# Mixture-of-experts layer on one core: full expert tiles first, each expert's last tile after them, and the padding rows written during the expert phase

## The reference

```
x = x + cross_attention(layernorm(x), ctx)
xf = layernorm(x)
scores = softmax(xf @ gate_w.T)               # 32 experts
tw, ti = top_k(scores, 4);  tw /= tw.sum()    # 4 experts for each token
rg, ru = xf @ Rg.T, xf @ Ru.T
for e in range(32):                           # only the tokens that chose e count
    g = silu(rg @ Ug[e].T @ Cg[e].T);  u = ru @ Uu[e].T @ Cu[e].T
    y += w_e * ((g * u) @ Rd.T @ Ud[e].T @ Cd[e].T)
x = x + y + shared_expert(xf)
```

## Time and profile before

| | |
|---|---|
| time, median of 3 runs | 877.85 us (876.92 to 878.13) |
| time of the profiled execution | 878.0 us |
| its span, first to last instruction | 876.3 us |
| PE busy, share of the span | 777.2 us, 89% |
| POOL busy, DVE busy | 482.0 us, 593.4 us |
| first block | 0 to 407.3 us |
| expert phase, then combine phase | from 407.4 us to some 752 us, then to 876.3 us |

### The profile page before, as it was taken

The page is one execution under the profiler, slowest core; times in us unless marked ns, Lnnn a source line. Parts: engine busy times, 40 slices in busy tenths (PEclk is TensorE's granted clock), DMA queues, the critical chain, the costliest instruction groups (busy, mean ns, idle before and its releaser), DMA issues.

```text
span 876.3 us, 22261 instructions
## 1 busy us (share of the span) xinstructions
PE 777.2 (89%) x6034; PEld 639.1 (73%) x6035; DVE 593.4 (68%) x2017; ACT 469.4 (54%) x1411; POOL 482.0 (55%) x684
## 2 busy tenths in 40 slices
PE   4899999999999999632999999999999999999995
PEld 2566666666666666422898998899899898888884
DVE  2578888888888888540565666566566566477887
ACT  2678888888888888411444444444444443322331
POOL 0126566666666666570455555555555556576665
PEclk9999999999999999855999999999999999999998
DMA  6345655555555555776344444344344342577875
GB/s 193 101 121 168 177 168 172 178 169 178 175 167 169 172 172 178 236 193 180 116 132 127 123 129 130 121 127 131 120 127 131 120 130 98 189 247 236 257 243 179
DMA packets 101889, 142.01 MB, mean 162 GB/s; under 512 B 16171, under 2 KB 83043, under 8 KB 101219
## 3 DMA queue, kind: packets, MB, share of 16 engines
q1 hardware_dynamic: 87395, 101.18, 39.3%
q0 software_dynamic: 14080, 38.89, 12.7%
q10 hardware_dynamic: 384, 1.58, 0.7%
HBM read 86.73 MB, written 58.82 MB: 166 GB/s over the span
## 4 chain that ended last, share of the span: by engine, by line
PE 39%; DMA 4%; issue 4%; DVE 3%; POOL 2%; SPq 1%; POOLq 0%; DVEq 0%; ACT 0%
PE bank L1197 9%; PE bank L1205 8%; PE bank L1219 6%; PE bank L1221 6%; PE bank L1230 4%; PE bank L1212 4%; DMA got<-yt_d 2%; DVE acc L1394 2%; DMA x2t<-xn2t_d 1%; PE bank L1268 1%; PE bank L1248 1%; POOL scaled L1330 1%; PE bank L1259 1%; PE bank L1255 1%; DVE wts L1399 1%
## 5 line engine op out<-in xcount | busy, mean ns | idle before, releaser
L1319 POOL DMA_INDIRECT yt_d<-yo,name_i x160 | 157.7, 986 | 28.7 <-issue 22.5
L740 POOL DMA_INDIRECT xs_d<-rgu,sloti x128 | 127.5, 996 | 41.7 <-issue 31.6
L1197 PE MATMUL bank<-down_w,rdt 128*128 x320 | 97.7, 387 | 19.8 <-issue 18.7
L1364 DVE TENSOR_TENSOR h<-bank,gated 128x176 f32<-128x176 f32 x160 | 54.7, 342 | 86.8 <-ACT gated L1283 86.8
L1317 POOL TENSOR_TENSOR fence<-ones 128x1 f32<-128x1 f32 x160 | 29.4, 184 | 140.6 <-DVE name_i L1354 140.4
L1205 PEld LDWEIGHTS bank<-ht,rd_w 88*128 88x128 f32 x640 | 96.7, 192 | 8.2 <-issue 0.3
L1279 ACT ACTIVATE rdt<-bank 128x128 f32<-128x128 f32 x160 | 44.3, 277 | 104.6 <-PE bank L1205 104.5
L1205 PE MATMUL bank<-ht,rd_w 88*128 88x128 f32 x640 | 97.7, 275 | 0.0
L1283 ACT ACTIVATE gated<-bank 128x176 f32<-128x176 f32 x160 | 50.7, 317 | 87.1 <-PE bank L1221 87.1
L1353 DVE COPY yo<-bank 128x256 f32<-128x256 f32 x160 | 67.3, 420 | 26.0 <-PE bank L1197 25.9
L1359 DVE COPY ht<-bank 88x256 f32<-88x256 f32 x160 | 67.3, 420 | 21.4 <-PE bank L1212 12.2
(11 more groups left out here) (163 smaller groups left out, 1928.0 us busy)
## 6 DMA issues: line engine op xcount, KB each, us to landing
xg<-xs_d SPq DMA_DIRECT2D x160, 128.5 KB, 2.1
got<-yt_d SPq DMA_DIRECT2D x32, 512.0 KB, 4.2
raw<-in_raw SPq DMA_DIRECT2D x32, 496.0 KB
v<-v SPq DMA_DIRECT2D x128, 34.0 KB, 2.0
xs_d<-in_spare SPq DMA_DIRECT2D x4, 1028.0 KB, 7.4
xin<-in_x SPq DMA_DIRECT2D x32, 128.0 KB
ctxt<-in_ctxt SPq DMA_DIRECT2D x32, 128.0 KB, 3.9
xres<-in_x SPq DMA_DIRECT2D x32, 128.0 KB
```

Source lines behind the costliest of these rows:

```text
L740: nc.gpsimd.indirect_dma_start(xs_d, bass.IndirectOffsetOnAxis(sloti[:, b, k:k + 1], 0), rgu[:, b, k, :], None)\
L1197: nc.tensor.matmul(y_ps[b], rdt[:, b, :], weight(down_w, DOWN), start=True, stop=True)\
L1319: nc.gpsimd.indirect_dma_start(yt_d, bass.IndirectOffsetOnAxis(name_i[:, b, :], 0), yo[:, b, :], None)\
```

## The change

The table of tiles has a new order. Its first 128 entries are for full tiles of all experts, expert after expert, with the tiles of an expert now rounded down; entries that this leaves over point to spare rows. The last 32 entries are one tile for each expert, the last one, which holds what remains and padding. The first part is worked out as before, but over 128 entries, so that PE turns two columns and not four; the second part is three small DVE instructions, put where DVE waits for PE.

The padding rows leave the first block. The new function `fill_tail` issues one of the 32 transfers in each of the first 16 steps of the expert phase on SP and one on POOL (16 each), in front of what that step did before. SP waits for all 32 before it loads entry 128. ACT issues none.

```diff
-    tails(sp, mybir.EngineType.SP, 0, 3 * GROUP, tail_out[0])
-    sp.wait_ge(tail_out[0], 16 * 3 * GROUP)
...
-    tails(act, mybir.EngineType.Activation, 3 * GROUP, 3 * GROUP, tail_out[1])
-    act.wait_ge(tail_out[1], 16 * 3 * GROUP)
...
-    tails(pool, mybir.EngineType.Pool, 6 * GROUP, EXPERTS - 6 * GROUP, tail_out[2])
-    pool.wait_ge(tail_out[2], 16 * (EXPERTS - 6 * GROUP))
...
-for k in range(2 * KT):
-    m = nc.tensor.matmul(bank6[0:1, k * P:(k + 1) * P], found[:, k // KT, k % KT].unsqueeze(1),
+for k in range(2):
+    m = nc.tensor.matmul(bank6[0:1, k * P:(k + 1) * P], found[:, k:k + 1],
                          ident[:, :], start=True, stop=True)
...
-nc.vector.tensor_copy(counts[:, :], free[0:1, :]).then_inc(counts_done, 1)
 step(nc.vector.tensor_tensor(total_f[:, :], free[:, :], ebase[:, :], ALU.subtract))
-step(nc.vector.tensor_scalar(total_f[:, :], total_f[:, :], float(P - 1), None, ALU.add))
...
+nc.vector.tensor_copy(counts[:, :], free[0:1, :])
+nc.vector.tensor_copy(table[:, 0, LOOK + FULL:LOOK + ETILES], eiota[0:1, :])
+nc.vector.scalar_tensor_tensor(out=table[:, 1, LOOK + FULL:LOOK + ETILES], in0=tiles_f[0:1, :],
+                               scalar=float(P), in1=ebase[0:1, :], op0=ALU.mult, op1=ALU.add)
 dve.wait_ge(found_psum, 1)
...
+def fill_tail(eng, engine, s, first):
+    if not isinstance(s, int) or s >= EXPERTS // 2:
+        return
+    if s % GROUP == 0:
+        free_row[engine] = entries(engine, counts, first + s, GROUP, DUMP - P,
+                                   "a region's base and at most TOKENS tokens")
+    dst = xs_d[bass.ds(free_row[engine][s % GROUP], P), :].rearrange("(a b) d -> a (b d)", a=16)
+    eng.dma_start(dst, a["tails"][first + s]).then_inc(tail_out[engine], 16)
...
     def expert(s, ph):                                        # SP
+        fill_tail(sp, mybir.EngineType.SP, s, 0)
...
-    run_experts(sp, expert)
+    pipeline(sp, 2 * AHEAD, FULL, FULL, AHEAD, expert)
+    for out in tail_out.values():
+        sp.wait_ge(out, 16 * EXPERTS // 2)
+    with sp.Fori(0, (N - FULL) // AHEAD) as g:
+        for u in range(AHEAD):
+            expert(g * AHEAD + (FULL + u), u)
...
     def expert(s, ph):                                        # POOL
+        fill_tail(pool, mybir.EngineType.Pool, s, EXPERTS // 2)
```

More of the change, by code:

```diff
@@ L49 @@
 DUMP = EXPERTS * CAP
-SPARE = ETILES - TOKENS * TOPK // P
+FULL = TOKENS * TOPK // P
+SPARE = ETILES - FULL
 LN_EPS, RMS_EPS = 1e-5, 1e-6
@@ L294, in build @@
             KT = -(-ETILES // P)
+            assert FULL == P and SPARE == EXPERTS
             total_f = asb("total_f", [P, EXPERTS])
@@ L300, in build @@
             tile_no = asb("tile_no", [P, KT])
[L301 to L308, removed]
+            over = asb("over", [P, EXPERTS])
+            skipped = asb("skipped", [P, EXPERTS])
+            owner = asb("owner", [P, 1])
+            start = asb("start", [P, 1])
+            row = asb("row", [P, 1])
+            found = asb("found", [P, 2])
+            ld_no, found_done, found_psum = (asem(n) for n in ("ld_no", "found_done", "found_psum"))
             chain = asem("chain")
-            tail_out = [asem(f"tail_out{k}") for k in range(3)]
             def at_step(s, n):
@@ L316, in build @@
             with nc.Block() as block:
[L317 to L328, removed]
                 @block.sync
@@ L1037, in _ @@
                                                       ALU.mult, ALU.add))
[L1038 to L1042, removed]
@@ L1043, in _ @@
-                    step(nc.vector.tensor_reduce(owner[:, :], over[:, :, :], AX.X, ALU.add))
-                    step(nc.vector.tensor_reduce(start[:, :], skipped[:, :, :], AX.X, ALU.add))
-                    step(nc.vector.tensor_tensor(start[:, :], tile_no[:, :], start[:, :], ALU.subtract))
+                    step(nc.vector.tensor_tensor(over[:, :], ends[:, :], tile_no[:, 0:1].broadcast_to([P, EXPERTS]),
+                                                 ALU.is_le))
+                    step(nc.vector.tensor_tensor(skipped[:, :], over[:, :], tiles_f[:, :], ALU.mult))
@@ L1047, in _ @@
+                    step(nc.vector.tensor_reduce(owner[:, :], over[:, :], AX.X, ALU.add))
+                    step(nc.vector.tensor_reduce(start[:, :], skipped[:, :], AX.X, ALU.add))
+                    step(nc.vector.tensor_tensor(start[:, :], tile_no[:, 0:1], start[:, :], ALU.subtract))
                     step(nc.vector.tensor_scalar(start[:, :], start[:, :], float(P), None, ALU.mult))
+                    nc.vector.tensor_scalar(found[:, 0:1], owner[:, :], float(EXPERTS - 1), None, ALU.min)
@@ L1048, in _ @@
                     step(nc.vector.scalar_tensor_tensor(out=row[:, :], in0=owner[:, :], scalar=float(CAP),
                                                         in1=start[:, :], op0=ALU.mult, op1=ALU.add))
-                    nc.vector.tensor_scalar(found[:, 0, :], owner[:, :], float(EXPERTS - 1), None, ALU.min)
-                    nc.vector.tensor_scalar(found[:, 1, :], row[:, :], float(DUMP + (SPARE - 1) * P), None,
-                                            ALU.min)\
+                    nc.vector.tensor_scalar(found[:, 1:2], row[:, :], float(DUMP + (SPARE - 1) * P), None, ALU.min)\
@@ L1054, in _ @@
                         .then_inc(found_done, 1)
+                    nc.vector.tensor_copy(counts[:, :], free[0:1, :])
+                    nc.vector.tensor_copy(table[:, 0, LOOK + FULL:LOOK + ETILES], eiota[0:1, :])
+                    nc.vector.scalar_tensor_tensor(out=table[:, 1, LOOK + FULL:LOOK + ETILES], in0=tiles_f[0:1, :],
+                                                   scalar=float(P), in1=ebase[0:1, :], op0=ALU.mult, op1=ALU.add)
                     dve.wait_ge(found_psum, 1)
                     step(nc.vector.tensor_copy(
-                        table[:, :, LOOK:LOOK + ETILES],
@@ L1058, in _ @@
-                        bank6[0:1, :].rearrange("p (c t) -> p c t", c=2)[:, :, 0:ETILES]))
+                        table[:, :, LOOK:LOOK + FULL],
+                        bank6[0:1, 0:2 * P].rearrange("p (c t) -> p c t", c=2)))
                     nc.vector.memset(sup_w[:, :, SHARED:SPAD], 0.0)
@@ L1100, in build @@
             TURN, UP, HTURN, RDOWN, DOWN, LAG = 3, 5, 7, 9, 11, 12
+            tail_out = {mybir.EngineType.SP: esem("tail_out0"), mybir.EngineType.Pool: esem("tail_out1")}
+            free_row = {}
+            def fill_tail(eng, engine, s, first):
[6 more added lines that the diff above has]
+                eng.dma_start(dst, a["tails"][first + s]).then_inc(tail_out[engine], 16)
             def run_experts(eng, body):
```

## The result

The changed kernel takes 868.53 us (median of 4 runs, 867.92 to 868.9) beside 877.38 us for the kernel before: a ratio of 0.9907, interval 0.9884 to 0.9930. That is 8.9 us less by the medians, 8.2 us by the ratio; 867.9 us had been forecast. The profiled execution took 868.9 us, its span 867.2 us. The sum came out, but two of its terms did not; their errors point in opposite directions and cancel in part.

What follows compares the result with a forecast made beforehand. Padding sets the seam between the blocks; behind it PE bounds the expert phase. -13.5 + 1.4 + 2.1 = -10.0 us from the profiled 878.0 gives 868.0, so 867.9 us at the median; range 864.4 to 871.5 us (8 in 10).

Steps and rivals of the forecast that it cites:

- The seam: Between first block and expert phase: without the padding wait, the second block begins 13.5 us earlier, at 393.9 us.
- the late one: Rival at the first block's end: scatters, not padding, landed late all along; 877 us, no change; chance 0.04.
- the shorter seam: Rival at the seam: POOL's 2.0 us drain shrinks and DVE sets the seam; 866.7 or 864.4 us; chance 0.05.
- The first load: Expert phase start on SP: first table reading 1.4 us later, xg of tile 0 issued 2.5 us into the block.
- The later loads: SP's loads for tiles 1 to 8: issued 1.24 us apart instead of 0.5, plus counts and table every four tiles.
- Traffic in front of the loads: Expert phase start: padding on the shared DMA engines delays PE 2.1 us beyond the 1.4, between 0.7 and 5.
- about 18 as the sign: Expert phase start: PE takes tile 8 about 18 us behind the barrier instead of 15.9.
- The halves: SP's and POOL's queues share DMA time equally: tile 6 lands at 16.4 us at the latest, 3.9 us late.
- The clock: Rival at the expert phase start: late loads keep PE at 1.2 GHz until padding is written; 883 us; chance 0.04.
- My own mark for being wrong: Expert phase start: the prediction is wrong if PE's clock rises later than 8 us after its first transposes.
- Another sign: Expert phase loads: the longest landing of xg is well above 2.5 us only among the first nine.
- The order of tiles: Expert phase: the new order changes no size, with 160 tiles, same products and weights already in SBUF; nothing.

Runs made afterwards that it cites:

- warm(11): Changed kernel plus 11 unused PE products before the expert phase and 4 before the waits for tiles 1 and 2: 868.09 us, ratio 0.9891.

## Why the prediction was right, by its steps

**The seam** was right. From the last scatter's issue to the barrier it is 18.3, 18.8 and 17.3 us in the old order and 4.3 us in the profile after: some 13.8 us, 13.5 forecast. The scatter landed 2.6 us after its issue (2.4 forecast), so it had not been the late one; POOL's drain took 1.4 us instead of 2.0; DVE's drain lay at 392.1 us, 0.8 us ahead of POOL's pass. Of the shorter seam, the rival, that is the small part which came true.

**The first load** was right: issued 397.00 - 394.6 = 2.4 us behind the barrier, 2.5 forecast.

**The later loads** were issued at 9.4 us (tile 4) and 16.3 us (tile 8), 8.9 and 15.3 forecast: right in kind, up to 1 us short. Part of that is a slip: by my own terms, 1.24 + 0.7 + 0.9 us for the steps to tiles 4 and 8, they come out at 9.1 and 15.6 us.

**Traffic in front of the loads** was mis-sized. Beyond the 1.4 us I took 2.1 us with an upper end of 5, and it was 5.5: some 3.6 us up to tile 4, the last tile whose load PE waits for, and 2.0 us of low clock behind it. Tile 8 came at 22.9 us, where I had named about 18 as the sign. I had shared DMA time between two queues as if only their sums counted. The runs show another thing: early loads bear POOL's whole traffic for 0.3 us at most, late ones do not. SP's padding costs 3.5 us alone, by late issue, and leaves the loads no lead to hide a landing of 4 us behind. The halves to which the Trainium skill's rule led (DMA: Bandwidth & Descriptors, Issuing engines are not separate DMA queues) gave at most 3.9 us. Tile 6, for which I had worked that out, did land inside it, at 15.0 us (16.4 at the latest); but PE had lost 5.0 us by tile 4, and did not make them up. In the same section the Trainium skill says that issuing from several engines saves only sequencer time, usually small beside the transfer. Here SP's sequencer was the costly place, and the same padding from POOL was nearly free.

**The clock**, a rival at 4 in 100, took part without deciding: 1.2 GHz until 413.8 us, for 2.0 us and not for 15. My own mark for being wrong, a rise later than 8 us after the first transposes, was passed by 6 us. The rise of before, which I had put at some 4 us, took some 5 by its rows. Another sign failed without harm: loads of 4 us and more to land came behind tile 9 too (4.5 us for those issued near 421 us), but PE did not wait for them.

**The order of tiles** I put at nothing, and 1.4 us came with it. They stand in PE's waits at the head of its loop of 8. Between 480 and 700 us (total, times, longest), before, with the new order alone, and in the changed kernel with `warm(11)`:

```profile
PE bank L1197 <- issue: 14.3, 14, 1.1
```
```profile
PE bank L1201 <- issue: 12.2, 13, 1.0
```
```profile
PE bank L1201 <- issue: 11.9, 13, 0.9
```

That is 1.02, 0.94 and 0.92 us each. One by one they have a pattern; the first rows of the same stretch, before and with the new order alone:

```profile
482.00 0.69 PE L1197 MATMUL bank<-down_w,rdt 128*128 x2 [1.15 <-issue]
498.51 0.69 PE L1197 MATMUL bank<-down_w,rdt 128*128 x2 [0.91 <-issue]
515.23 0.69 PE L1197 MATMUL bank<-down_w,rdt 128*128 x2 [1.11 <-issue]
```
```profile
495.08 0.69 PE L1201 MATMUL bank<-down_w,rdt 128*128 x2 [0.91 <-issue]
511.66 0.69 PE L1201 MATMUL bank<-down_w,rdt 128*128 x2 [0.97 <-issue]
528.17 0.69 PE L1201 MATMUL bank<-down_w,rdt 128*128 x2 [0.91 <-issue]
```

Before, every second wait is 0.2 us longer; with the new order, every third is 0.05 us longer. Over the some 18 heads of the phase that is about 9 x 0.2 - 6 x 0.05 = 1.5 us, an estimate from these rows, and enough for the whole difference. With `warm(11)` the table is the same, but only PE's program has more products in it, and the pattern is gone. So the pattern can change with PE's program alone, and PE's program is another in the new order too: it has two products fewer in front of the loop. That the order of the tiles shortens anything is not shown. What in the program lengthens a wait stays open.

Together: -13.8 + 6.9 - 1.4 = -8.3 us, against 8.2 to 8.9 measured. The mechanism, a seam won and a start partly lost, was right; that the forecast of 867.9 us came as near as it did was luck in part. An extra cost of 3.4 us met 1.4 us that I had not expected and a median of before that lay 0.5 us lower in these runs; the rest is within the scatter of single executions.

**The best version** leaves the change as it is and moves SP's padding 16 steps later: 862.04 us, ratio 0.9841, some 6 us better than the changed kernel. Moving POOL's too makes no difference that can be told.

## What to carry to other kernels

A wait for background writes at the seam of two phases is worth taking out, but the place they move to must not be the queue that starts the next phase: put them behind the first loads, or on an engine that has nothing to issue yet. When costing it, count the issues in front of each load before the bytes, and ask how much lead the loads have left. A sum that comes out right is no proof of its terms: read each term in the profile.

## What the hardware showed beyond that

Thirteen DRAM-to-DRAM transfers of 128.5 KB raised the landing of loads from 2.1 to 4.0 us (medians of the runs without and with them) with the DMA engines at 0.98, and PE lost nothing: tile 8 came at 16.3 us in both. In the start of the expert phase PE's clock was worth nothing with early loads (16.4 us at 2.4 GHz, 16.3 us with the rise on the way) and 2.0 us with late ones. The waits at the head of PE's loop, 0.91 to 1.15 us each, account for the 1.4 us between two kernels whose loops have the same products.
